# Value products of two head pairs in one group of TensorE work, one shared distance table, and a new order of the side work

## The reference

```python
x = x + 0.5 * ffn(layernorm(x))
x = x + attention(layernorm(x))     # 16 heads of 64, causal
x = x + 0.5 * ffn(layernorm(x))
# ffn: h = relu(x @ W_fc.T)**2 ; y = h @ W_proj.T ; five steps of a spiking neuron on y,
#      mem = 0.9*mem + y - (mem > 1), the output is the number of spikes / 5
# attention: sim = (q*SCALE) @ k.T - |i-j|*slope[h] ; softmax over j <= i ; out @ w_out + b_out
```

## Time and profile before

| | us |
|---|---|
| median of three runs (1609.4 to 1611.03) | 1609.67 |
| the profiled execution | 1611.76 |
| its span, first to last instruction | 1610.0 |

### The profile page before, as it was taken

One profiled execution on the slowest core, in us unless ns is written; L12 is line 12 of the kernel. 1 busy time (PEld: TensorE's weight loads), 2 busy tenths in 40 slices (PEclk: granted clock), 3 DMA queues, 4 the chain that ended last, 5 costly groups with the idle time before them and its releaser, 6 DMA issues.

```text
span 1610.0 us, 33997 instructions
## 1 busy us (share of the span) xinstructions
PE 1558.1 (97%) x10376; PEld 1253.8 (78%) x10376; DVE 1288.1 (80%) x4344; ACT 1312.4 (82%) x3485; POOL 954.2 (59%) x1253
## 2 busy tenths in 40 slices
PE   6899999999999999999999999999999999999996
PEld 5778778788787878778788787878778788787775
DVE  6586797878879788797878879788797878878765
ACT  6788888888888888888888888888888888888882
POOL 2555656666566666656666566666656666665551
PEclk8999999999999999999999999999999999999998
DMA  2454544444545444544444545444545444545440
GB/s 87 99 109 102 112 96 105 106 100 101 119 96 112 104 94 102 119 96 105 106 100 103 116 96 115 104 92 102 119 96 107 104 104 101 109 96 109 106 89 14
DMA packets 80052, 163.12 MB, mean 101 GB/s; under 512 B 12800, under 2 KB 30848, under 8 KB 79744
## 3 DMA queue, kind: packets, MB, share of 16 engines
q1 hardware_dynamic: 79872, 160.94, 46.4%
HBM read 6.88 MB, written 4.19 MB: 7 GB/s over the span
## 4 chain that ended last, share of the span: by engine, by line
PE 86%; DVE 9%; issue 2%; POOL 1%; ACT 1%; DMA 0%; POOLq 0%; DVEq 0%; SPq 0%; ACTq 0%
PE bank L445 16%; PE bank L459 14%; PE bank L431 11%; PE bank L432 10%; PE bank L411 7%; PE bank L415 7%; PE bank L412 7%; PE bank L504 7%; DVE xn L687 3%; PE bank L487 2%; PE bank L517 2%; PE bank L515 2%; PE bank L514 2%; DVE negsc L654 2%; POOL rstd L1102 1%
## 5 line engine op out<-in xcount | busy, mean ns | idle before, releaser
L1089 POOL TENSOR_TENSOR prob<-prob,rsum 128x512 f32<-128x512 f32 (+3 forms) x1024 | 769.9, 767 | 489.5 <-DVE rsum L663 486.9
L936 ACT ACTIVATE prob<-negsc,negmax 128x512 f32<-128x512 f32 (+3 forms) x1024 | 574.4, 563 | 165.7 <-DVE negmax L654 163.3
L654 DVE CUSTOM_DVE_ANT_0 negsc<-bank,alibi 128x512 f32<-128x512 f32 (+3 forms) x1024 | 466.9, 475 | 0.3 <-PE bank L432 0.3
L947 ACT COPY probT<-bank 128x512 f32<-128x512 f32 x640 | 352.0, 584 | 27.5 <-PE bank L445 21.4
L445 PE MATMUL bank<-ident,prob 128*128 128x128 f32 x2560 | 350.9, 273 | 0.8 <-POOL prob L1089 0.5
L431 PE MATMUL bank<-keys,queries 128*128 128x256 f32 (+2 forms) x1024 | 348.6, 351 | 0.3
L663 DVE RECIPROCAL rsum<-sums 128x1 f32<-128x1 f32 (+1 forms) x768 | 122.3, 159 | 260.1 <-PE bank L432 248.0
L432 PE MATMUL bank<-keys,queries 128*128 128x256 f32 (+2 forms) x1024 | 320.0, 324 | 0.0
L445 PEld LDWEIGHTS bank<-ident,prob 128*128 128x128 f32 x2560 | 299.4, 140 | 24.0 <-POOL prob L1089 0.7
L459 PE MATMUL bank<-probT,vals 128*64 128x512 f32 (+3 forms) x2048 | 303.9, 439 | 3.3 <-DVE queries L778 2.5
L459 PEld LDWEIGHTS bank<-probT,vals 128*64 128x64 f32 x2048 | 135.6, 136 | 163.6 <-issue 125.2
(11 more groups left out here) (108 smaller groups left out, 2421.0 us busy)
## 6 DMA issues: line engine op xcount, KB each, us to landing
queries<-queries SPq DMA_DIRECT2D x381, 256.0 KB, 3.0
keys<-k_lo SPq DMA_DIRECT2D x254, 128.0 KB, 2.7
keys<-keys SPq DMA_DIRECT2D x127, 128.0 KB, 3.1
x_in<-in_L_attn_x_dram SPq DMA_DIRECT2D x16, 256.0 KB, 3.1
out_dram<-x SPq DMA_DIRECT2D x15, 256.0 KB, 3.6
prob<-in_L_attn_w_qkv_dram SPq DMA_DIRECT2D x1, 1536.0 KB, 9.4
prob<-in_L_attn_w_out_dram SPq DMA_DIRECT2D x1, 512.0 KB, 10.2
probT<-in_L_ffn_W_fc_dram SPq DMA_DIRECT2D x1, 256.0 KB, 3.3
```

The lines of the kernel that those rows point to most:

```text
L654: ins = dve.tensor_tensor_reduce(negsc[:, k % 3, col:col + WIDTH[i]], src, alibi[:, 2 * p + h, N - WIDTH[i]:N], 1.0, MASKED, ALU.add, ALU.min,
L936: ins = act.activation(prob[:, p % 2, h, PCOL[i]:PCOL[i] + WIDTH[i]], negsc[:, k % 3, col:col + WIDTH[i]], ACT.Exp, bias=negmax[:, p % 2, ...
L947: act.copy(probT[:, turn_slot(p, t), :], turn_bank[(len(TRUNS) * p + t) % 2][:, :]).then_inc(s_turned_out, 1)
L1089: ins = pool.tensor_tensor(pr, pr, rsum[:, p % 2, seg:seg + 1].to_broadcast([P, WIDTH[i]]), ALU.mult)
```

## The change

`alibi`, sixteen tables of 512 distances, each multiplied by a slope, becomes one table `dist`. The slope becomes the scale of the DVE instruction at line 654, and the query weights are divided by the slopes (16 small instructions in place of one, in ACT and in DVE, in the head of the program). The room goes to `probT`, whose ring holds 20 places. The value products of pairs s-3 and s-2 are now made one right after the other, in slots 1, 3, 5 and 7. The order of the side work is new throughout. In the tables only the new lines stand here; of `PEORDER` and `ACTORDER`, all of whose rows change, the rows for slots 0, 4, 5 and 6 of the first.

```diff
-TRING = 10
+TRING = 20
 TBEAT = [
+    [1, 2, 3, 4, 4],
+    [1, 4, 4, 5, 5],
+    [1, 4, 4, 5, 5],
+    [1, 1, 4, 4, 5],
+    [3, 3, 4, 5, 5],
+    [0, 2, 2, 5, 5],
+    [1, 1, 4, 4, 5],
+    [0, 2, 2, 5, 5],
 ]
-ACCBEAT = [7, 6, 6, 6, 6, 6, 11, 11]
-OUTEV = (2, 1)
+ACCBEAT = [11, 15, 6, 17, 8, 11, 6, 8]
+OUTEV = (2, 3)
 PEORDER = [
+    ["TAD", "TAD", "ATD", "ATD", "TAD", "ATD"],
...
+    ["DAT", "ATD", "TAD", "TDA", "TAD", "ATD"],
+    ["ADT", "TDA", "ATD", "ATD", "ATD", "ADT"],
+    ["ADT", "ATD", "TAD", "ADT", "ATD", "TAD"],
...
 SIDE = [
+    (0, 0, "q", 0, 0), (0, 1, "v", 0, 0), (0, 2, "v", 1, 0), (0, 2, "k", 0, 0), (0, 3, "t1", 0, 1),
+    (0, 5, "fc1", 0, 1), (0, 5, "fc1", 1, 1),
+    (1, 1, "q", 0, 0), (1, 2, "k", 0, 0), (1, 4, "pv", 0, 0), (1, 4, "pv", 1, 0),
+    (2, 0, "q", 0, 0), (2, 1, "fc1", 2, 1), (2, 2, "k", 0, 0), (2, 3, "fc1", 3, 1), (2, 4, "v", 2, 0),
+    (2, 4, "ot", 0, -1),
+    (3, 0, "v", 3, 0), (3, 0, "k", 0, 0), (3, 1, "q", 0, 0), (3, 3, "pv", 0, 0), (3, 3, "pv", 1, 0),
+    (3, 5, "v", 4, 0),
+    (4, 0, "y1", 0, 1), (4, 0, "k", 0, 0), (4, 1, "y1", 1, 1), (4, 1, "t3", 0, -1), (4, 2, "q", 0, 0),
+    (4, 3, "fc3", 0, -1), (4, 4, "fc3", 1, -1), (4, 5, "fc3", 2, -1), (4, 5, "v", 5, 0),
+    (5, 1, "k", 0, 0), (5, 1, "q", 0, 0), (5, 3, "fc3", 3, -1), (5, 4, "pv", 0, 0), (5, 4, "pv", 1, 0),
+    (6, 0, "q", 0, 0), (6, 0, "k", 0, 0), (6, 3, "y3", 0, -1), (6, 3, "v", 6, 0), (6, 4, "y3", 1, -1),
+    (6, 4, "t2", 0, 1), (6, 5, "v", 7, 0),
+    (7, 1, "q", 0, 1), (7, 2, "k", 0, 1), (7, 4, "pv", 0, 0), (7, 4, "pv", 1, 0),
 ]
+SPIKE1 = [(4, 2), (4, 3), (4, 3), (4, 4), (4, 5), (4, 5), (4, 5), (4, 5), (5, 1), (5, 2), (5, 2), (5, 3), (5, 3), (5, 4)]
+SPIKE3 = [(7, 1), (7, 1), (7, 4), (7, 4), (7, 4), (8, 2), (8, 3), (8, 5), (9, 1), (9, 2), (9, 3), (9, 4), (9, 4), (9, 4)]
+LN1 = dict(stats=(0, 0), aggregate=(0, 1), rstd=(0, 2), normalise=(0, 2))
+LN2 = dict(stats=(5, 4), aggregate=(6, 2), rstd=(6, 3), normalise=(6, 4))
+LN3 = dict(stats=(3, 0), aggregate=(3, 1), rstd=(3, 1), normalise=(3, 2))
...
+        def pv_pair(b, s, i):
+
+            return before(b, s, 3 - i)
...
+        def acc_at(p):
+
+            return divmod((p - p % 2 + 3) * BEATS + ACCBEAT[p], BEATS)
...
                 elif kind == "pv":
                     for j in PVORDER:
-                        pv(bank or side_bank[n % 2], *before(b, s, 2), j)
+                        pv(bank or side_bank[n % 2], *pv_pair(b, s, i), j)
...
-                                                   alibi[:, 2 * p + h, N - WIDTH[i]:N], 1.0, MASKED, ALU.add, ALU.min,
+                                                   dist[:, N - WIDTH[i]:N], SLOPES[2 * p + h], MASKED, ALU.add, ALU.min,
...
-                act.mul(wq_hi[:, :], w_raw[:, 0:INNER], -SCALE).then_inc(s_whi, 1)
+                for h in range(HEADS):
+                    ins = act.mul(wq_hi[:, h * DH:(h + 1) * DH], w_raw[:, h * DH:(h + 1) * DH], -SCALE / SLOPES[h])
+                ins.then_inc(s_whi, 1)
...
-                for h in range(HEADS):
-                    ins = act.mul(alibi[:, h, :], dist, SLOPES[h])
-                ins.then_inc(s_alibi, 1)
```

More of the change, by code:

```diff
@@ L290, in last_user @@
                 s, _, kind, i, off = SIDE[m]
[L291 removed]
+                if m % 2 == n % 2 and off in offsets and (kind != "pv" or pv_exists(b, s, i)):
                     return freed(kind, i, b + off, s)
@@ L559, in slot @@
                         if part == "A":
-                            for back in (3, 2):
-                                if ACCBEAT[(s + 2 - back) % PAIRS] == k + BEATS * (back - 2) and exists(*before(b, s, back)):
-                                    accumulate(*before(b, s, back))
+                            for p in range(PAIRS):
+                                if acc_at(p) == (s, k):
+                                    accumulate(b, p)
+                                elif acc_at(p) == (s + PAIRS, k) and b > 0:
+                                    accumulate(b - 1, p)
                         elif part == "T":
@@ L568, in slot @@
                             for n, kind, i, off, _ in side_at(s, k, offsets):
-                                if kind == "pv" and not exists(*before(b, s, 2)):
+                                if kind == "pv" and not pv_exists(b, s, i):
                                     continue
@@ L847, in slot @@
                     for n, kind, i, off, ss in side_at(s, k - 1, offsets):
-                        if kind == "pv" and not exists(*before(b, ss, 2)):
+                        if kind == "pv" and not pv_exists(b, ss, i):
                             continue
```

90 lines of the change are left out of this document (38 added, 52 removed), and 13 rows, old and new, of the table SIDE.

## The result

The changed kernel takes 1630.44 us (median of four runs, 1629.57 to 1634.28) against 1609.86 for the kernel before on the same chip: ratio 1.013, 95% interval 1.0117 to 1.0144. It is 21 us slower, where I had forecast 23 us faster.

A forecast was written before the change was run, and what follows sets the result against it. TensorE, busy 97% of the span, was taken as the bound. 1610 (span) - 22 (places) - 4 (waits over 14 blocks) + 3 (ends) = 1587 us, range 1570 to 1610.

The forecast's parts named there:

- The saving by places: Entering and leaving half-array value products costs TensorE 0.35 us a place; 63 fewer places save 22 us.
- The table: One scaled table costs nothing: line 654 keeps its mean, and GpSimd's wait covers the head's small VectorE instructions; 0 us.
- the three waits to be removed: TensorE waits in each block: `t2` for `xn` 0.71, slot 6's first scores for keys 0.31, `t1` for a bank 0.17; -1.19 us.
- Waits that the new order makes: Step walking each block's beats for new TensorE waits; with the removals, -0.3 us a block, -4 us over 14 blocks.
- the turn in (5, 2): Turns wait for norms behind VectorE's four spike instructions in (4, 5): 0.2 to 1.5 us, taken as 0.6 a block.
- keys: Keys landing late before slots 1 and 5: 0.2 us a block, up to 1.5.
- +0.1 for `t1`: At (0, 3), VectorE's work up to `normalise` and `xn` against TensorE's 3.3 us before `t1`: +0.1 us a block.
- two value products at one place: Two copies and two `att_lo` meet, but the banks' next users are at least a beat and 1.35 us away: 0.
- rival 1: VectorE's burst at (4, 5) gives all back, deciding from 1.9 us more waiting a block; chance of ending slower 0.10.
- a wait of 2.2 us and 1609: Rival 1's mechanism: spike instructions hold GpSimd off, norms 1.6 us later, wait 2.2 instead of 0.6; +22 us, 1609.
- The ends: Tail, block 15 and block 0 together: +2 for SPIKE3's rest, +2 for block 15's `k`, -1 for block 0; +3 us.
- waits anyway: -1: Block 0 has fewer side jobs and waits in any case: -1 us.

The follow-up runs named there:

- e6_split: The kernel before, with turns made in the middle of value products in five beats of a block, nothing else moved: 1662.54 us, ratio 1.0319.
- e11_light_after: The changed kernel with the spiking-neuron instructions in the blocks on 128 of 512 columns, a measuring tool: 1584.57 us, ratio 0.9841.
- e1_table: The kernel before with only the one scaled distance table and the weights of the change: 1612.28 us, ratio 1.0008.
- e8_t2: The kernel before with the last four first-neuron spike instructions up to two beats earlier and second-norm statistics a little earlier: 1610.48 us, ratio 0.9997.
- e13_third_light: The changed kernel with only the third neuron (SPIKE3) on 128 of 512 columns: 1616.08 us, ratio 1.0034.
- e14_first_light: The changed kernel with only the first neuron (SPIKE1, with its burst) on 128 of 512 columns: 1598.5 us, ratio 0.9928.
- the light kernels: The kernel before and the changed kernel, each with spiking-neuron instructions in the blocks on 128 of 512 columns: 1608.93 us before, 1584.57 us changed.
- e9_keys: The changed kernel with `k` of slot 1 in (1, 1) in place of (1, 2): 1629.59 us, ratio 1.012.
- e2_spread: The changed kernel with SPIKE1 spread, two instructions in (4, 5) instead of four, and second-norm statistics moved to (6, 0): 1627.87 us, ratio 1.0107.
- e15_fewer: The changed kernel's side work and value products, 11 VectorE instructions a neuron in place of 14, GpSimd adding the held sum, beats new: 1635.63 us.
- e12_even: The changed kernel's merged value products, with spikes, bias addition and keys moved to even VectorE out, all work kept: 1630.43 us, ratio 1.0125.
- e16_early: The changed kernel with `y1` a slot earlier, first neuron in (3, 3) to (5, 4), and other work moved: 1707.11 us, ratio 1.0607.
- e5_mended: e2_spread with third-neuron beats moved, slot 2's `k` in (2, 1), and two heads' low query weights made ahead of `xn`: 1627.61 us, ratio 1.0102.

## Why the prediction was wrong

**The saving by places was right.** I took 0.35 us a place; e6_split measures 0.30. At 63 places that is 19 us in place of 22. That a second pair follows without a gap held (e11_light_after).

**The table was right**: nothing, e1_table. In the head the first scores come later in e1_table as in the changed kernel (39.2 and 38.3 against 36.5 us), but in e1_table the first output transpose is only 0.2 late: block 0 has waits that take it up. I had said that GpSimd's wait would cover the sixteen small VectorE instructions. Beside them its addition of 128x4 took 2.12 us in seven of the profiled executions and 0.22 in the four others, with the same program in the head; where it took 0.22 the first scores came at 36.2 to 36.7. So this late start comes and goes among the profiled executions, and is no mark of the new order. What decides it is not known.

**Of the three waits to be removed two were there.** `t2` (0.71) and `t1` (0.17) wait in each block before. The 0.31 before the first scores of slot 6 I had read in block 3 and taken for all; in the eleven other blocks from 2 to 13 these scores start 0.24 behind the product before, which is no wait. So the term was 0.88 and not 1.19. In the changed kernel `t2` no longer waits. e8_t2 shows that a removal is not yet a gain: in the kernel before, too, the wait of `t2` can be removed, and 0.1 us of its 0.71 is gained.

**The step that failed is "Waits that the new order makes".** It was a sum of places, each priced alone: +0.6 for the turn in (5, 2), +0.2 for keys, +0.1 for `t1`, 0 for "two value products at one place". Forecast per block, with the removals: -0.3, so 96.54 - 4 x 0.35 - 0.3 = 94.85. Measured: 97.27. The 2.4 us between them, times 14, are 34 of the 43 us by which I was wrong. 0.2 of the 2.4 is the price of a place and 0.3 the keys that did not wait. The rest is this step: with four places at 0.30 and 0.9 us of waits gone the block would be 94.4, so the new waits cost 2.8 us where I had 0.9, and 2.96 goes when both neurons are light. In detail:
- *(5, 2).* My chain gave 7.2 us for VectorE and GpSimd against 6.1 for TensorE, 1.1, and I then took 0.6 "with each lag at its full length". The rows give 489.39 - 481.37 = 8.0 against 6.8, so 1.18. The discount had no row behind it; but that the full 1.1 comes out is luck, since both sides of it were 0.7 to 0.8 too short. I had 0.8 us for a spike instruction; beside GpSimd's squares and a norm three of the four take 1.04, 1.20 and 1.42, and only the last, beside an idle GpSimd, 0.68. An estimate from these rows: at the pace of the last, 0.60 from start to start, the four would take 2.4 us in place of 4.25, and the 1.85 less is more than the 1.18 that was lost. So the stretching beside GpSimd may be what turned a full beat into a wait; no run here has the same work without it.
- *(5, 4).* "At least a beat and 1.35 us away. 0." The user of the bank was two beats away, but its reader on ScalarE stood behind exponentials that waited for VectorE. 0.5 us.
- *(0, 3) and (2, 0).* I had looked for `xn` there and taken +0.1, and for (2, 0) nothing. Together with what lies between they cost 0.87 by e13_third_light.
- *Keys.* 0.2 was the right size (2.5 us in twelve blocks), though the listing has them in five single places.

What joins the first three is the point that I missed in my own first paragraph. I read 83% for VectorE as slack, and gave rival 1 a chance of 0.10 to end slower because "elsewhere it has slack of three tiles". That share is a mean over slots. The change puts 14 instructions of the first neuron into (4, 2) to (5, 4), where they had lain in (2, 4) to (6, 1), and the third neuron into slots 7 to 1. I had added up VectorE's work only for (4, 2) to (4, 5), up to one wait. It had to be followed beat by beat through the whole stretch, for each result that TensorE or ScalarE takes from it. Rival 1 was the right mechanism ("at the four spike instructions of (4, 5)"), and decided from 1.9 us; e14_first_light gives 2.11 for the first neuron.

**The page.** I had cited the Trainium skill ("SBUF — State Buffer", Who interferes with whom) for VectorE and GpSimd taking turns at a shared port, and by it a wait of 2.2 us and 1609. The burst agrees with the mechanism (0.68 alone, 1.42 beside a square, and the squares 1.49 where 1.04 is the mean before). The wait was 1.18 and not 2.2, because GpSimd had just two squares and one norm to do and then sat idle for 1.30 us (its row above): the delay came by VectorE's `recip`, and not by a queue on GpSimd.

**The ends.** Forecast +3; the span says 9.6 + 3.3 = 12.9. Between the light kernels the same sum is +2.9 (6.7 ahead and 3.8 less behind the steps). With `ot`'s own shift taken out (4.2, and 3.2 in the light ones) the end is 7.5 longer in the one case and 0.6 shorter in the other, so that part goes with the neurons; I had put it at +2, for `SPIKE3`. (In e9_keys, whose end is the changed kernel's, it is 5.0 longer: the 7.5 has some of the one execution in it.) The head is 5.4 longer, and still 3.5 between the light kernels: that part is not VectorE's neurons. 1.8 of the 5.4 is the late start of the first scores (above). Another part is that block 0 has no value products in slot 1, and so nothing over the landing of the keys. The first scores of its slot 2, and the window behind them:

```profile
60.05 0.77 PE L441 MATMUL bank<-keys,queries 128*128 128x512 f32 x1 [3.88 <-issue]
```

```profile
60.00:65.00 5.00, 4.95 (x15) 4.11 (x15) 1.99 (x7) 2.00 (x5) 1.95 (x4) 0.50 0.12 26
```

I had written that block 0 "waits anyway: -1". In four other profiled executions with `k` in (1, 2) (e2_spread, e11_light_after, e13_third_light, e14_first_light) this wait is 2.6.

**What stays open.** No kernel here has the merged value products, all of the work, and a gain. e15_fewer and e12_even moved the waits; e16_early failed on banks. That such an order exists is likely by e14_first_light and not shown. Open too is how the loss divides between VectorE's work and its stretching beside GpSimd.

## What to carry to other kernels

For a new order, follow each helping engine's work beat by beat from the beat at which its input is there to the beat at which the result is due, before pricing any single wait. An engine's busy share slot by slot tells where to look, and no more: 99% stood beside a loss in two slots, 98% and 100% beside none in two others, and 90% beside a loss of some 3 us. A wait read once has to be looked up in the other blocks. To learn whether an engine takes back a gain, make its instructions narrow in both kernels and time both: the pair of light kernels answered what mending single places (e2_spread, e5_mended) had not. A removed wait is a gain only where the work behind it isn't late for the same reason.
